# A recommendation tower's ramp: one store of all codes, loads in another order, and half 1 and 2's picks regrouped

## The reference

```python
    # _L0_rec_ref(xl=e, x0=r_x0, w, alpha, hv); b = 2048, s = 16, f = 39, d = 16
    A = jnp.repeat(x0, s, axis=1)
    Bm = jnp.repeat(xl, f, axis=2).reshape(b, s * f, d)
    out = jnp.einsum('bnh,bnd,nk,khd,kd->bkh', A, Bm, alpha, w, hv[..., 0])
...
z = _L0_rec_ref(e, r_x0, L0_rec_w, L0_rec_alpha, L0_rec_hv)   # e: tbl_0[ids[:, 0]] to tbl_15[ids[:, 15]]
z = z.reshape(z.shape[0], -1)
h = jnp.concatenate([z, dense_ctx], axis=1)
h = jnp.maximum(h @ W_top1 + b_top1, 0.0)                     # 272 -> 512
h = jnp.maximum(h @ W_top2 + b_top2, 0.0)                     # 512 -> 256
y = h @ W_top3                                                # 256 -> 1
```

## Time and profile before

| | |
|---|---|
| time of three runs | 180.37 us median (179.28 to 182.56) |
| the profiled execution's own time | 178.92 us |
| its span, first to last instruction | 177.0 us |
| busy: PE, DVE, POOL, ACT | 164.0, 142.5, 110.9, 66.0 us |
| share of the chain that ended last: PE, DMA, DVE | 69%, 13%, 4% |

### The profile page before, as it was taken

The page is one execution under the profiler, slowest core; times in us unless marked ns, Lnnn a source line. Parts: engine busy times, 40 slices in busy tenths (PEclk is TensorE's granted clock), DMA queues, the critical chain, the costliest instruction groups (busy, mean ns, idle before and its releaser), DMA issues.

```text
span 177.0 us, 5041 instructions
## 1 busy us (share of the span) xinstructions
PE 164.0 (93%) x2131; PEld 124.3 (70%) x2131; DVE 142.5 (80%) x177; ACT 66.0 (37%) x176; POOL 110.9 (63%) x116
## 2 busy tenths in 40 slices
PE   6549898968997999999999999999999999999993
PEld 1338696736984879696969696969686967776671
DVE  2978797893799999999899979996999899495000
ACT  3440788084881125212431243123403341451141
POOL 2777777777747777777777777777777776000000
PEclk9999999996999999999999999999999999999999
DMA  5889999999999997989498948694559360000000
GB/s 87 307 120 327 246 275 161 270 373 264 283 334 250 345 320 150 363 248 230 79 352 240 216 160 300 189 230 104 183 219 222 48 231 6 2 4 0 0 4 0
DMA packets 15085, 34.26 MB, mean 194 GB/s; under 512 B 6618, under 2 KB 10582, under 8 KB 11990
## 3 DMA queue, kind: packets, MB, share of 16 engines
q1 hardware_dynamic: 10162, 31.51, 58.9%
q0 software_dynamic: 3584, 0.92, 6.6%
q10 hardware_dynamic: 1316, 1.50, 2.9%
HBM read 33.88 MB, written 0.04 MB: 192 GB/s over the span
## 4 chain that ended last, share of the span: by engine, by line
PE 69%; DMA 13%; DVE 4%; ACT 3%; SPq 3%; issue 3%; POOL 3%; DVEq 0%
PE bank L927 17%; PE bank L842 17%; PE bank L848 15%; PE bank L894 11%; DMA ids_half_dram<-ids_half 6%; PE bank L915 5%; PE bank L835 4%; DMA ids_b<-ids_half_dram 3%; POOL e L478 3%; DMA e<-tbl_dram,ids_all 3%; DVE prod L642 2%; SPq L446 2%; DMA ids_all<-ids_dram 1%; ACT apart L724 1%; PE bank L856 1%
## 5 line engine op out<-in xcount | busy, mean ns | idle before, releaser
L478 POOL DMA_INDIRECT e<-tbl_dram,ids_all x112 | 110.7, 988 | 38.7 <-issue 33.2
L642 DVE TENSOR_TENSOR prod<-x,bank 128x2048 f32<-128x2048 f32 x40 | 90.3, 2279 | 8.8 <-issue 4.6
L927 PE MATMUL bank<-prod,m_w 128*32 128x256 f32 x640 | 38.6, 382 | 2.5 <-DVE prod L642 2.5
L894 PE MATMUL bank<-table,onehot 125*128 125x64 bf16 (+1 forms) x288 | 31.9, 198 | 2.3 <-DVE low L537 2.3
L842 PE MATMUL bank<-tower,w_z 128*128 128x256 f32 x128 | 32.8, 403 | 0.7 <-ACT tower L743 0.7
L894 PE MATMUL bank<-low,onehot 125*128 125x64 bf16 (+1 forms) x288 | 31.8, 197 | 0.0
L894 PE MATMUL bank<-rest,onehot 125*128 125x64 bf16 (+1 forms) x288 | 31.8, 199 | 0.0
L894 PEld LDWEIGHTS bank<-table,onehot 125*128 125x128 bf16 x288 | 27.4, 98 | 5.7 <-issue 2.9
L927 PEld LDWEIGHTS bank<-prod,m_w 128*32 128x32 f32 x640 | 19.1, 109 | 17.0 <-issue 3.5
L848 PE MATMUL bank<-tower,w 128*128 128x256 f32 x128 | 30.7, 382 | 0.1
L842 PEld LDWEIGHTS bank<-tower,w_z 128*128 128x128 f32 x128 | 24.2, 199 | 6.3 <-ACT tower L743 3.1
(11 more groups left out here) (60 smaller groups left out, 85.4 us busy)
## 6 DMA issues: line engine op xcount, KB each, us to landing
x<-x_dram SPq DMA_DIRECT2D x16, 1024.0 KB, 8.1
x<-x_dram SPq DMA_DIRECT2D x16, 512.0 KB, 12.4
ids_b<-ids_half_dram SPq DMA_DIRECT2D x7, 576.0 KB
e<-tbl_dram,ids_all POOLq DMA_INDIRECT x112, 4.7
prod<-windows_c_dram ACTq DMA_DIRECT2D x1, 768.0 KB
prod<-windows_c_dram ACTq DMA_DIRECT2D x1, 512.0 KB, 5.6
w_z<-w_z_dram SPq DMA_DIRECT2D x1, 512.0 KB
w<-w_dram SPq DMA_DIRECT2D x1, 512.0 KB, 11.0
```

The costliest lines, as they stand in the source:

```text
L478: nc.gpsimd.indirect_dma_start(out=e[:, tile, f * D:(f + 1) * D], out_offset=None, in_=t[f"tbl_{f}"][:, :], in_offset=bass.IndirectOffsetO ...
L642: nc.vector.tensor_tensor(prod[:, s % NPROD, :].rearrange("p (q b) -> p q b", q=HP), x0[:, tile % NX, :].rearrange("p (q b) -> p q b", q=H ...
L894: made = nc.tensor.matmul(o_bank[i % 2][:, at:at + m * D], onehot[:, n % 2, g, HOT.index(f), tile * P:(tile + 1) * P], parts[part][:, KT_A ...
L927: made = nc.tensor.matmul(z_bank[q * ZW:(q + 1) * ZW, a * HB:(a + 1) * HB], m_w[:, UNIT_OF[g], hp * ZW:(hp + 1) * ZW], prod[:, s % NPROD, ...
```

## The change

- One DMA stores the codes of all halves. Before, one stored half 1's codes, and six more stood behind the x0 loads of half 0.
- SP's list behind that is reordered: half 2's codes are loaded right behind half 0's x0 tiles, then x0 tile 3, the context, the first tower weight, x0 tile 4, half 3's codes, the second tower weight.
- Half 1's hot fields are regrouped: fills 4, 5, 6 hold fields {1,2,4}, {5,12,15}, {7,10,13} and not {4,7,10,13}, {15,1,2}, {5,12}. So the first window part of half 1 needs fills 4 and 5 only (`kept_at`).
- On DVE the first plane of half 2 is made ahead of product 3, and half 1's masks of fills 5 and 6 stand ahead of product 4; their sums stay behind it.
- On PE half 0's last windows are turned ahead of pick 5, and picks 7 and 8 (half 2's first) stand ahead of half 0's last contraction (4).
- On ACT `spread_e(1, 0)` stands ahead of `keep_z(0)`, `spread_e(1, 1)` behind it, and `make_plane(3)` one step later.

```diff
+SECOND_FILLS = [[[1, 2], [4]], [[5, 12], [15]], [[7, 10, 13]]]
...
-PLANE_STEPS = {1: [0, 0], 2: [4, 4], 3: [5, 6], **{n: [UH * (n - 1) - 4, UH * (n - 1) - 3] for n in range(4, NH)}}
-PICK_STEPS = {1: [BEFORE, 2, 3], 2: [5, 5, 6], 3: [9, 10, 11], **{n: [UH * (n - 1) - 2, UH * (n - 1) - 1, UH * (n - 1)] for n in range(4, NH)}}
+PLANE_STEPS = {1: [0, 0], 2: [2, 2], 3: [5, 6], **{n: [UH * (n - 1) - 4, UH * (n - 1) - 3] for n in range(4, NH)}}
+PICK_STEPS = {1: [BEFORE, 2, 3], 2: [4, 4, 5], 3: [9, 10, 11], **{n: [UH * (n - 1) - 2, UH * (n - 1) - 1, UH * (n - 1)] for n in range(4, NH)}}
...
-    return 2 * p + 2 if n == 0 else FIRST_FILLS[n + 1]
+    return 2 * FILL_PACK[j] + 2 if n == 0 else FIRST_FILLS[1] + 2 if (n, j) == (1, 0) else FIRST_FILLS[n + 1]
...
-            sp.dma_start(ids_rows[1], ids_half[1:IDS:NH, :]).then_inc(ids_stored[0], 16)
+            sp.dma_start(ids_rows.rearrange("n f b -> f n b"), ids_half[:]).then_inc(ids_stored, 16)
...
             load_x0(1)
             load_x0(2)
-            for n in range(2, NH):
-                sp.dma_start(ids_rows[n], ids_half[n:IDS:NH, :]).then_inc(ids_stored[1], 16)
+            load_ids(2)
             sp.dma_start(b_w3[:], t["b_w3"]).then_inc(in_b_w3, 16)
+            load_x0(3)
             load_ctx()
             sp.dma_start(w1_z[:], t["w1_z"].rearrange("(a p) n -> p a n", p=P)).then_inc(in_w1, 16)
-            sp.wait_ge(ids_stored[1], 16 * (NH - 2))
-            load_ids(2)
-            load_x0(3)
+            load_x0(4)
             load_ids(3)
             sp.dma_start(w2[:], t["w2"].rearrange("(a p) n -> p a n", p=P)).then_inc(in_w2, 16)
-            load_x0(4)
...
-                for i in KEEPS.get(s, []):
+                for i in KEEPS[4] if s == 3 else KEEPS.get(s, []) if s != 4 else []:
                     mask_rows(i)
...
                 if s == 4:
+                    spread_e(1, 0)
                     keep_z(0)
-                    spread_e(1, 0)
+                    spread_e(1, 1)
...
                 if s == 5:
                     find_apart(3)
+                elif s == 6:
                     make_plane(3)
...
                 if s == 2:
                     for unit in CONTRACTS[2]:
                         contract(unit)
+                    turn_windows(0, 2)
                     for i in PICKS[2]:
                         pick_rows(i)
                 if s == 4:
-                    for unit in CONTRACTS[4]:
-                        contract(unit)
+                    contract(CONTRACTS[4][0])
+                    for i in PICKS[4]:
+                        pick_rows(i)
+                    contract(CONTRACTS[4][1])
+                    turn_windows(1, 0)
                     pe.wait_ge(in_ctx, 16 * N_CTX_LOADS)
                     pe.wait_ge(in_w1, 16)
                     for job in JOBS[4]:
                         fill_t(job)
+                turn_windows(1, 1)
```

More of the change, by code:

```diff
@@ L69 @@
 HALF_FILLS = [[[4, 7, 10, 13]], [[15], [1, 2]], [[5, 12]]]
-FILLS = [(_n, _runs) for _n in range(8) for _runs in (FRONT_FILLS if _n == 0 else HALF_FILLS)]
+SECOND_FILLS = [[[1, 2], [4]], [[5, 12], [15]], [[7, 10, 13]]]
+FILLS = [(_n, _runs) for _n in range(8) for _runs in (FRONT_FILLS if _n == 0 else SECOND_FILLS if _n == 1 else HALF_FILLS)]
 FIRST_FILLS = {_n: 0 if _n == 0 else len(FRONT_FILLS) + (_n - 1) * len(HALF_FILLS) for _n in range(9)}
@@ L170, in act_planes_by, with kept_at @@
     return sum(of <= n for of in ACT_HALVES)
-def kept_at(n, p):
-    return 2 * p + 2 if n == 0 else FIRST_FILLS[n + 1]
+def kept_at(n, j):
+    return 2 * FILL_PACK[j] + 2 if n == 0 else FIRST_FILLS[1] + 2 if (n, j) == (1, 0) else FIRST_FILLS[n + 1]
 PE_IDS = 1
@@ L307, in program @@
         in_small = sem("in_small")
-        ids_stored = [sem(f"ids_stored_{n}") for n in range(2)]
+        ids_stored = sem("ids_stored")
         in_ids_b = {n: sem(f"in_ids_b_{n}") for n in range(PE_IDS, NH)}
@@ L439, in _ @@
             load_x0(0)
-            sp.wait_ge(ids_stored[0], 16)
+            sp.wait_ge(ids_stored, 16)
             load_ids(1)
@@ L652, in _ @@
                     sum_rows(3)
-                for i in KEEPS.get(s, []):
+                for i in KEEPS[4] if s == 3 else KEEPS.get(s, []) if s != 4 else []:
                     mask_rows(i)
-                if s != 4:
-                    for plane in PLANES.get(s, []):
-                        make_plane(*plane)
+                for plane in PLANES.get(s, []):
+                    make_plane(*plane)
                 for i in KEEPS.get(s, []):
@@ L660, in _ @@
                 if s == 4:
-                    for plane in PLANES[4]:
-                        make_plane(*plane)
                     dve.wait_ge(in_b_w3, 16)
@@ L692, in spread_e @@
             def spread_e(n, j):
-                act.wait_ge(rows_kept, kept_at(n, FILL_PACK[j]))
+                act.wait_ge(rows_kept, kept_at(n, j))
                 for i in range(j + 1):
@@ L802, in _ @@
                     make_plane(2)
-                if g in (0, 1) and s > 0:
+                if g in (0, 1) and s not in (0, UH):
                     spread_e(n, g + 1)
@@ L998, in _ @@
                         fill_t(job)
-                if s == 1 or g == 2:
+                    turn_windows(1, 1)
+                if s == 1 or g == 2 and n > 0:
                     turn_windows(n, g)
-                elif g == 4 and n + 1 < NH:
+                elif g == 4 and 0 < n < NH - 1:
                     turn_windows(n + 1, 0)
-                fills = PICKS.get(s, []) if s > 2 else []
+                fills = PICKS.get(s, []) if s > 2 and s != 4 else []
                 units = CONTRACTS.get(s, []) if s not in (0, 2, 4) else []
@@ L1017, in _ @@
                         pick_rows(i)
[L1018 to L1022, removed]
+                if s in (UH, 2 * UH):
                     for i in fills:
```

## The result

The changed kernel takes 181.23 us (median of 20 runs, 179.23 to 186.38); the kernel before, run beside it, 179.65 (median of 20, 177.52 to 184.46). The ratio is 1.0092, with a 95% interval of 1.0056 to 1.0128: slower by 0.9%, where 1.5% faster was forecast. The profiled execution took 180.81 us, its span is 179.0. Executions of one kernel differ by some per cent, so every ratio here compares the faster group of both kernels' executions, medians are of all of them, and the traces of `codes_early`, `codes_early_list` and the second `drain`, which fell outside that group, are not read.

What follows compares the result with a forecast made beforehand. The start of product 5 was taken to set when PE's unbroken stretch begins. Starting it 2.67 us earlier, with picks and moved loads at nothing, gave 2.7 us: 180.37 to 177.7 (profiled execution 178.92 to 176.2), range 176.0 to 180.0.

Steps and rivals of the forecast that it cites:

- The codes' landing: Half 2's codes, loaded behind x0 tile 2, land at 33.7 us; lower bound 31.8, upper 33.4 to 34.3.
- DVE: DVE's work up to product 5: product 3 at 34.5, product 4 at 37.9, product 5 at 42.65, 2.67 us earlier.
- PE in the same time: PE up to contraction 7: picks 7 and 8 cost nothing ahead of contraction 4; PE's unbroken stretch begins 2.7 us earlier.
- Moved loads: Loads now later in SP's list: no wait taken, up to 1 us as the other end; bigger store at most 0.3.
- From product 5 to contraction 7: DVE's unchanged list takes 8.21 us to product 7 at 50.86; contraction 7 follows 2.34 later, at 53.2.
- Quicker codes: Half 2's codes land at 33.0 or less; gain about 3.3 to 4.0 us, time 176.4 to 177.1; chance 0.17.
- The clock stays low: Clock falls as before, tower group costs 1.62 us more, 0.8 of it lost: 178.5; chance 0.12.
- Second half of the list late: Half 3's codes or second weight 1 us late, costing up to 1 us: gain 1.7, time 178.7; chance 0.14.
- Slower: Half 2's plane and picks 7, 8 delay half 0's work, one for one beyond codes at 33.7; chance 0.06.
- The likeliest case: Product 5 near 42.65, contraction 7 near 53.2: gain 2.7 us, median time 177.7.

Runs made afterwards that it cites:

- codes_early: Changed kernel with SP's list behind half 2's codes as context, first weight, x0 tile 3, half 3's codes, second weight, x0 tile 4; ratio 1.0013.
- codes_early_list: Kernel before with one store and half 3's codes and the second weight loaded ahead of x0 tile 4, old engine streams; ratio 0.9991.
- drain: Changed kernel, x0 tile 3, half 3's codes, second weight held until product 2 is done, tile 4 until product 4; ratios 0.987, 0.991 (176.85, 177.44 us).
- ctx_first: Changed kernel with the context and the first tower weight loaded ahead of x0 tile 3; ratio 1.003 (0.990 to 1.016).
- streams_only: Changed kernel with the old stores and the old list of SP, so only the engines' streams are new; ratio 1.022 (1.009 to 1.035).

## Why the prediction was wrong, step by step

- **The codes' landing**: forecast 33.7, bound 31.8; 30.03 in the profile, 32.38 in the first `drain`, 32.81 in `ctx_first`. The order behind x0 tile 2 holds, but that tile itself landed at 28.64 and not at 31.8. The bound had been taken from a trace in which six stores followed it. And it was no floor in that trace either: the prediction read the last of these stores as a sign that nothing passes the tile, but the store, queued behind it, was down at 30.83 and the tile at 31.8.
- **DVE**: right. From product 3 to product 4, 3.30 us for a forecast 3.4. From product 3 to product 5, 8.38 us in `drain` for a forecast 8.15.
- **PE in the same time: "So the picks cost nothing here; their cover is the wait for product 4 and its sums."** This is the step that failed: a late supply of instructions was put at nothing. The cover was there (2.09 us in the run with the picks put back), but the sum assumed that PE can issue 84 matmuls whenever their data are there. It stopped behind the 16th. What it cost: without the stop, 84 picks from 36.45 take 2.83 us (`drain`: 36.97 to 39.80), and contraction 4, 1.07, and the turning, 0.74, put product 5 near 41.1. It came at 47.31, 6.2 later: 3.92 of the stop; 1.8 of the 68 picks behind it at the lower clock (4.10 us for 2.29, from `drain`'s rate); 0.4 of the contraction (1.50 for 1.07).
- Its root is in **"Moved loads"**: the sum asked of each load who uses it, and found slack. The instruction packets are in no list of the program, and when they come depends on it.
- **From product 5 to contraction 7**: forecast 42.65 to 53.2, 10.55 us; measured 10.57 in the changed kernel and 10.56 in `drain`. Behind 57 us PE was busy for 112.70 us of 113, as forecast. So the whole miss is in the start of product 5: 47.31 for 42.65 is 4.66 us, and the execution took 180.81 for 176.2.
- **The rivals.** "Quicker codes" had its condition (codes at 30.03, product 3 at 32.73) and none of its gain, since the stop came behind it. "The clock stays low" came true in effect (0.50 for 41 to 45.3), but it followed the stop and was priced at 0.8. "Second half of the list late" was right in `ctx_first` with 2.9 us for a price of at most 1: product 6 at 49.76, where 4.48 us behind product 5 would be 46.85. "Slower" had the right side for the wrong reason; `streams_only` shows that mechanism, with 49.14 for product 5 where one for one from 33.7 gives 42.65 + 5.1 = 47.75.
- The likeliest case (product 5 near 42.65, contraction 7 near 53.2) is what `drain` and `ctx_first` show for product 5 (41.57, 42.37), and `drain` for contraction 7 (52.13). The medians gave 1.9 to 2.5 us of the 2.7, but with the old streams as well (2.1 and 2.2), in which product 5 starts at 43.88 and 43.17 for 45.32 before and the clock stays at 1.00 too. So the runs show a gain for the list with its loads held back; for the regrouped streams, which the prediction counted into the 2.7, they show none.

## What to carry to other kernels

Ahead of moving loads to the front, look where the instruction packets of the busiest engine lie in the trace: count its instructions by the packet, see how many microseconds a packet has between its start and its seam, and take that as one more load with a due time. A stop behind an instruction that waits for nothing, at the same instruction number in each execution, was a late packet here; a few dummy instructions ahead of it tell. The cure here was to issue prefetches later, not earlier, tied to the work ahead of their use.

## What the runs showed of the hardware that had not been expected

- PE stopped for 0.23 to 4.08 us at recorded instructions that lie 256 apart (961, 1217, 1473), where its packet was late.
- PE went on 1.31 to 1.65 us behind the end of the packet, in six traces with a stop ahead of number 961.
- After a stop of 3.92 us the clock stood at the lower level from 39.14 us for 6.83 us, two microseconds of it before PE began to work again.
